# A state-space layer and a retrieval layer in one kernel: convolution inputs for two tiles at once, with W_in's columns stationary

## The reference

```python
zxbcdt = u @ W_in                                   # [4096, 2320]
z, xBC, dt = split(zxbcdt)                          # 1024, 1280, 16 columns
conv = conv_b
for i in range(4):                                  # causal convolution along the tokens
    conv = conv + pad(xBC)[:, i:i + s] * conv_w[i]
x, B, C = split(silu(conv))                         # 1024, 128, 128
dt = softplus(dt + dt_bias)
y = ssd(x * dt, -exp(A_log) * dt, B, C) + x * D     # scan over the tokens
y = rmsnorm(y * silu(z)) * norm_scale
x1 = layernorm(u + y @ W_out)
h = silu(x1 @ W_up.T + b_up) @ W_down.T + b_down    # 512 -> 2048 -> 256
sx, ix = top_k(first half of q(h) . keys, 8)        # 8 heads, 64 keys a half
sy, iy = top_k(second half of q(h) . keys, 8)
sc, experts = top_k(sx + sy, 8)                     # 64 experts a token
z = silu((h . down_embed[experts]) * softmax(sc))
out = layernorm(x1 + sum_k z_k * up_embed[experts_k])
```

## Time and profile before

| | |
|---|---|
| time, median of 3 runs | 3190.46 us (3180.9 to 3191.35) |
| span of the profiled execution | 3168.2 us |
| median less that span | 22.3 us |
| PE busy | 2818.4 us, 89% |
| DVE busy | 2783.2 us, 88% |
| ACT busy | 2105.8 us, 66% |
| POOL busy | 2098.0 us, 66% |
| gathers' share of the 16 DMA engines' span | 76.5% |

### The profile page before, as it was taken

One profiled execution on the slowest core, in us unless ns is written; L12 is line 12 of the kernel. 1 busy time (PEld: TensorE's weight loads), 2 busy tenths in 40 slices (PEclk: granted clock), 3 DMA queues, 4 the chain that ended last, 5 costly groups with the idle time before them and its releaser, 6 DMA issues.

```text
span 3168.2 us, 39919 instructions
## 1 busy us (share of the span) xinstructions
PE 2818.4 (89%) x9216; PEld 1501.1 (47%) x9216; DVE 2783.2 (88%) x10160; ACT 2105.8 (66%) x6641; POOL 2098.0 (66%) x2056
## 2 busy tenths in 40 slices
PE   7998999999899999999999999899899999998963
PEld 4444455545454545444445444444445454444431
DVE  3488999999989899999999899898999999898987
ACT  4476766767776667776666677666676666677642
POOL 0067666677667677666667767667766666766676
PEclk9999999999999999999999999999999999999986
DMA  8078888888888788888888888888888888888888
GB/s 289 16 265 277 276 270 269 274 283 289 275 270 267 261 282 293 279 281 269 269 275 300 263 277 280 265 268 291 270 278 275 271 275 290 282 279 275 269 296 280
DMA packets 189837, 856.45 MB, mean 270 GB/s; under 512 B 36192, under 2 KB 39392, under 8 KB 189088
## 3 DMA queue, kind: packets, MB, share of 16 engines
q0 software_dynamic: 163840, 805.44, 76.5%
q1 hardware_dynamic: 19104, 34.87, 3.2%
q10 hardware_dynamic: 6656, 13.60, 1.2%
HBM read 845.38 MB, written 8.39 MB: 269 GB/s over the span
## 4 chain that ended last, share of the span: by engine, by line
PE 57%; POOL 11%; DVE 10%; DMA 10%; ACT 6%; issue 6%; SPq 0%; DVEq 0%; ACTq 0%; POOLq 0%
PE bank L465 14%; POOL ring L279 11%; DMA ring<-embed,idx 10%; PE bank L508 8%; PE bank L362 7%; PE bank L481 6%; PE bank L342 5%; DVE bank L1166 4%; PE bank L496 4%; PE bank L444 3%; PE bank L371 3%; ACT xc L691 3%; DVE ring L1152 2%; PE bank L472 2%; ACT raw L688 1%
## 5 line engine op out<-in xcount | busy, mean ns | idle before, releaser
L279 POOL DMA_INDIRECT ring<-embed,idx x2048 | 2096.7, 1024 | 1057.9 <-issue 544.3
L1166 DVE SCALAR_TENSOR_TENSOR bank<-ring,coef,bank 128x512 f32<-128x512 f32 x1312 | 990.8, 755 | 7.4 <-issue 0.2
L1152 DVE SCALAR_TENSOR_TENSOR ring<-ring,hcur 128x256 f32<-128x256 f32 x2048 | 827.1, 423 | 185.7 <-DMA ring<-embed,idx 182.6
L508 PE MATMUL bank<-ring,diag_c 128*128 128x512 f32 x1344 | 668.8, 628 | 119.6 <-ACT diag_c L666 103.9
L657 ACT ACTIVATE coef<-prob,zp 128x1 f32<-128x1 f32 x2048 | 459.1, 293 | 456.1 <-DVE ring L1152 454.9
L465 PE MATMUL bank<-w_up,zs 128*128 128x512 f32 x1024 | 490.4, 630 | 69.2 <-ACT zs L779 65.8
L508 PEld LDWEIGHTS bank<-ring,diag_c 128*128 128x128 f32 x1344 | 246.6, 199 | 385.8 <-issue 224.9
L465 PEld LDWEIGHTS bank<-w_up,zs 128*128 128x128 f32 x1024 | 200.7, 201 | 329.7 <-issue 238.6
L997 DVE SCALAR_TENSOR_TENSOR xc<-raw,taps,xc 128x128 f32<-128x128 f32 x960 | 266.0, 351 | 53.8 <-ACT xc L691 53.8
L342 PE MATMUL bank<-w_in,ut 128*128 128x512 f32 (+1 forms) x768 | 285.1, 524 | 4.4 <-ACT seg L679 4.3
L666 ACT ACTIVATE diag_c<-cst,coef 128x128 f32<-128x128 f32 x672 | 234.8, 394 | 49.4 <-PE bank L508 38.9
(11 more groups left out here) (147 smaller groups left out, 3685.1 us busy)
## 6 DMA issues: line engine op xcount, KB each, us to landing
ring<-embed,idx POOLq DMA_INDIRECT x2048, 4.6
ring<-uT SPq DMA_DIRECT2D x4, 2048.0 KB, 14.3
ut<-uT SPq DMA_DIRECT2D x32, 256.0 KB, 6.5
zs<-u SPq DMA_DIRECT2D x32, 256.0 KB, 5.7
out<-acc SPq DMA_DIRECT2D x32, 256.0 KB, 4.7
w_up<-W_upT ACTq DMA_DIRECT2D x1, 4096.0 KB, 12.7
w_in<-W_in ACTq DMA_DIRECT2D x1, 2560.0 KB, 17.0
w_in<-W_in ACTq DMA_DIRECT2D x1, 2048.0 KB, 21.5
```

What stands on the lines that cost most here:

```text
L279: pool.indirect_dma_start(out=ring[:, k % RING, :], out_offset=None, in_=embed, in_offset=bass.IndirectOffsetOnAxis(ap=idx[:, half, k:k + ...
L508: m = pe.matmul(bank[SUM][:, :], diag_c[:, (len(PE_ROWS) * t + n) % DIAGS, :], ring[:, k % RING, DP:ROW], start=(n == 0), stop=(n == len(P ...
L1152: m = dve.scalar_tensor_tensor(out=ring[:, k % RING, 0:DP], in0=ring[:, k % RING, 0:DP], scalar=1.0, in1=hcur[:, :], op0=ALU.mult, op1=ALU ...
L1166: dve.scalar_tensor_tensor(out=total if n == len(DVE_ROWS) - 1 else running[:, :], in0=ring[:, k % RING, DP:ROW], scalar=coef[:, k:k + 1], ...
```

## The change

- xBC is computed for two tiles (256 tokens) at once, and directly with its columns on partitions: blocks of W_in are stationary and 256 columns of uT move. There are five parts of two blocks (x_part). Parts 0 and 1 of the tiles i+2 and i+3 are computed at the end of an even tile(i), parts 2, 3 and 4 at the start of the odd tile behind it. The turns and xbc_copy go.
- In even tiles state_in moves behind out_proj(0) and new(0) and waits for ACT's inputs of parts 0 and 1, whose banks it shares.
- The 45 taps of a pair become 15 steps of two instructions with 256 columns each, all in odd tiles; silu is applied to two tiles at once, and the copy of the last three columns stands behind it.
- Buffers are reused: xskip lies in raw, the picks' v1, v2, i1 and place in xdec, yT in seg, coef in zp, and the result of the back norm in total itself, which the store reads. The waits that this needs are added.
- uT is loaded for two tiles at once, when the last tile that used the one before has its z projection. The store of tile i-1 stands behind the load of u for tile i+1.
- dt_proj(3) and turn_dt(3) move into tile 0 behind key_scores, raw_dt(3) and softplus(1) behind numbers; the first gathers wait for dt_proj(3).
- Row 51, the fourth of group 16, is added by DVE instead of PE.

```diff
-PARTS = 3
+PARTS = 5
+NJ = NT // 2
+W2 = 2 * P
+EARLY = 2
-GROUPS = (..., "PPPD", "PP", "PDD", "PPPP", "D", "DDD", "PPPD", "D", "PDD")
+GROUPS = (..., "PPPD", "PP", "PDD", "PPPD", "D", "DDD", "PPPD", "D", "PDD")
+TAP_ORDER = [(p, j) for of in ((0, 1), (2, 3, 4)) for j in range(TAPS - 1) for p in of]
...
-            def load_ut(i):
-                sp.wait_ge(z_mm, 2 * i)
...
+            def load_ut(j):
+                sp.wait_ge(z_mm, 4 * j)
...
+            for i in range(NT):
+                if i % 2 == 0 and i // 2 + 1 < NJ:
+                    load_ut(i // 2 + 1)
+                if i + 1 < NT:
+                    load_u(i + 1)
+                if i > 0:
+                    store(i - 1)
...
+            pool.wait_ge(dt_mm, 2 * (NT // DTB))
             gathers(0, 0, True)
...
-            def xbc_proj(i, first, part):
-            def turn_xbc(i, first, part):
...
+            def x_part(j, part):
+                if part == 0:
+                    pe.wait_ge(ut_in, 16 * j + 16)
+                for n in range(2):
+                    c = DI + (2 * part + n) * P
+                    for k in range(KD):
+                        m = pe.matmul(bank[X_BANKS[part]][:, n * W2:(n + 1) * W2], w_in[:, k, c:c + P], uT_v[:, k, :],
+                                      start=(k == 0), stop=(k == KD - 1))
+                m.then_inc(xbc_mm, 1)
...
-            def state_in(i):
+            def state_in(i, early):
                 pe.wait_ge(dec_ok, 4 * i + 4)
+                if early:
+                    pe.wait_ge(tap_ok, PARTS * (i + 1) // 2 + EARLY)
...
# tile on PE
-                if ahead:
-                    xbc_proj(i + 1, False, 0)
...
-                    turn_xbc(i + 1, False, 2)
+                late = ahead and i % 2 == 1
+                early = i % 2 == 0 and i // 2 + 1 < NJ
+                if late:
+                    x_part((i + 1) // 2, 2)
+                    x_part((i + 1) // 2, 3)
                 turn_x1(i)
+                if late:
+                    x_part((i + 1) // 2, 4)
                 old(4, 5, 6)
...
                 old(18, 19)
-                if ahead:
-                    state_in(i + 1)
+                if early:
+                    x_part(i // 2 + 1, 0)
+                elif ahead:
+                    state_in(i + 1, False)
+                if ahead:
                     turn_y(i + 1)
+                if early:
+                    x_part(i // 2 + 1, 1)
                 old(20, 21)
                 if ahead:
                     out_proj(i + 1, False, 0)
                 new(0)
+                if early:
+                    state_in(i + 1, True)
                 if ahead:
                     out_proj(i + 1, False, 1)
...
# tile on ACT
-                if ahead:
-                    history(i + 1)
+                if late:
+                    inputs((i + 1) // 2, 2)
                 old(4)
-                if ahead:
-                    xbc_copy(i + 1, 0)
...
-                    inputs(i + 1, 0)
+                if late:
+                    inputs((i + 1) // 2, 3)
+                turn_x1(i)
                 old(5)
...
+                if late:
+                    inputs((i + 1) // 2, 4)
                 old(6)
...
                     state_decay(i + 1, range(NH // 2))
+                if early:
+                    inputs(i // 2 + 1, 0)
+                if ahead:
                     state_decay(i + 1, range(NH // 2, NH))
                     turn_y(i + 1)
+                if early:
+                    inputs(i // 2 + 1, 1)
...
# tile on DVE: taps_of(n, ...) runs steps of TAP_ORDER in odd tiles
+                old(4)
+                taps_of(0, 1)
+                old(5)
+                taps_of(2, 3)
+                old(6)
+                taps_of(4, 5)
                 old(7)
                 if ahead:
                     time_steps(i + 1)
+                taps_of(6, 7)
                 old(8)
+                taps_of(8, 9)
+                old(9)
+                taps_of(10, 11)
+                old(10)
+                taps_of(12)
+                old(11)
+                taps_of(13)
+                old(12)
                 private(i, first)
+                taps_of(14)
...
-                    dve.wait_ge(o_ok, t)
+                    dve.wait_ge(out_done, 16 * t + 16)
```

More of the change, by code:

```diff
@@ L246, in store @@
                 sp.wait_ge(o_ok, t + 1)
[L247 to L258, removed]
+                sp.dma_start(out[bass.ds(t, 1)].rearrange("t p c -> p (t c)"), total[:, :]).then_inc(out_done, 16)
+            for i in range(NT):
[5 more added lines that the diff above has]
+                    store(i - 1)
             store(NT - 1)
@@ L551, in tile @@
                 key_scores(i, 1)
+                if first:
+                    dt_proj(3)
+                    turn_dt(3)
                 if ahead:
@@ L579, in tile @@
                 new(1, 2, 3)
-            xbc_proj(0, True, 0)
-            xbc_proj(0, True, 1)
-            xbc_proj(0, True, 2)
-            turn_xbc(0, True, 0)
-            turn_xbc(0, True, 1)
-            turn_xbc(0, True, 2)
+            for part in range(PARTS):
+                x_part(0, part)
             pe.wait_ge(wz_in, 16)
@@ L597, in _ @@
             turn_dt(1)
-            state_in(0)
+            state_in(0, False)
             dt_proj(2)
@@ L683, in inputs @@
-            def inputs(i, b):
-                n = min(4, KC - 4 * b)
-                at = bank[XBC_BANKS[b]]
-                act.wait_ge(xbc_mm, 3 * i + b + 1)
-                act.activation(raw[:, 4 * b:4 * b + n, TAPS - 1:],
-                               at[:, 0:n * P].rearrange("p (a c) -> p a c", a=n), ACT.Copy).then_inc(raw_ok, 1)
-                for c in range(4 * b, 4 * b + n):
-                    m = act.activation(xc[:, c, :], at[:, (c % 4) * P:(c % 4 + 1) * P], ACT.Identity,
-                                       bias=cbias[:, c:c + 1], scale=taps[:, c, TAPS - 1:TAPS])
+            def inputs(j, part):
+                at = bank[X_BANKS[part]]
+                c0 = 2 * part
+                if part == 0 and j > 0:
+                    act.wait_ge(hist_ok, j)
+                    act.wait_ge(y_mm, 2 * j)
+                act.wait_ge(xbc_mm, PARTS * j + part + 1)
+                act.activation(raw[:, c0:c0 + 2, TAPS - 1:], at[:, :].rearrange("p (a c) -> p a c", a=2), ACT.Copy)
+                for n in range(2):
+                    m = act.activation(xc[:, c0 + n, :], at[:, n * W2:(n + 1) * W2], ACT.Identity,
+                                       bias=cbias[:, c0 + n:c0 + n + 1], scale=taps[:, c0 + n, TAPS - 1:TAPS])
@@ L861, in tile @@
                 turn_h(i)
+                if first:
+                    copy_dt(3)
                 if ahead:
@@ L898, in tile @@
                 new(3)
-            for b in range(3):
-                xbc_copy(0, b)
-            for b in range(3):
-                inputs(0, b)
+            for part in range(PARTS):
+                inputs(0, part)
             masked_steps(0, range(NH), True)
@@ L994, in convolve @@
                 else:
-                    dve.wait_ge(conv_ok, PARTS * (3 * i + j - 1) + part + 1)
-                for c in range(4 * part, min(4 * part + 4, KC)):
-                    m = dve.scalar_tensor_tensor(out=xc[:, c, :], in0=raw[:, c, j:j + P], scalar=taps[:, c, j:j + 1],
+                    dve.wait_ge(conv_ok, NTAP * i + TAP_AT[part, j - 1] + 1)
+                for c in range(2 * part, 2 * part + 2):
+                    m = dve.scalar_tensor_tensor(out=xc[:, c, :], in0=raw[:, c, j:j + W2], scalar=taps[:, c, j:j + 1],
                                                  in1=xc[:, c, :], op0=ALU.mult, op1=ALU.add)
@@ L1258, in tile @@
                 numbers(i)
+                if first:
+                    raw_dt(3)
+                    softplus(1)
                 if ahead:
@@ L1287, in _ @@
             time_steps(0)
-            for j in range(TAPS - 1):
-                for part in range(PARTS):
-                    convolve(0, j, part)
+            for part, j in TAP_ORDER:
+                convolve(0, j, part)
             dve.wait_ge(w_out_in, 16)
```

173 lines of the change are left out of this document (65 added, 108 removed).

## The result

The changed kernel takes 3205.1 us (median of 12 runs, 3188.6 to 3219.6), the kernel before 3190.9 in 12 runs beside it: a ratio of 1.0048, interval 1.0027 to 1.0069. It is half a per cent slower.

What follows compares the result with a forecast made beforehand. One loop through four engines, no engine alone, was taken to bound the kernel. A pair: -3.6 + 3.7 + 0 + 1.0 + 0.2 = +1.3 us; 15 pairs, +20 on the median 3190.5, gave 3210; range 3158 to 3245, the forecast's own 3200 to 3230.

Steps and rivals of the forecast that it cites:

- The signs that it named: Even tiles: new_state waits 3 to 4 us, DVE waits for gathers; odd: no DVE idle; periods near 91 and 99.
- Even tile, start: From the gather of row 15 to the start of private in even tiles: 3.6 us shorter.
- Even tile, end: After scan_gate in even tiles, new_state waits for the later state_in; the end of norm1 moves 3.7 us later.
- Odd tile, start: From norm1's end to private's start in odd tiles, DVE last: no change, between minus 1.5 and plus 0.8 us.
- PE's wait for h: PE waits 2 to 3 us for private's start, and half-speed work may follow: plus 1.0 us a pair.
- The moved row: Row 51's weigh, 0.76 us a tile on DVE, is hidden ahead of its wait for row 59: nothing.
- DMAs: ut's load, doubled, moves to the middle of even tiles: plus 0.2 us, between minus 1 and plus 0.7.
- Start and end: Tile 0's gain is taken back by softplus(1) on DVE; tiles 30 and 31 have no parts: 0, between -5 and +5.
- The base: Median 3190.5 us, to which the sum was added, with 22 us taken to lie around the profiled span of 3168.2.
- The shorter path wins: Rival: TensorE keeps 2.4 GHz through its wait, even tiles save 4.2 us; -2.0 a pair, 3160 us; chance 0.30.
- DVE sets the pace throughout: Rival: 60 taps become 30 of 0.41 us; -4.3 a pair, +1.5 for moved rows, 3148 us; chance 0.05.
- Saving and stall cancel: Rival: no clock term, +0.1 to +0.3 us a pair, 3194 us; chance 0.21.

Runs made afterwards that it cites:

- the first trace: The kernel before the change, unchanged, as first profiled: span 3168.2 us, where the median of its executions is 3190.9 us.
- The halves: Changed kernel with the first half of state_in put before x_part(0) and the second before x_part(1): 3139.9 us, ratio 0.9859 to the kernel before.
- the second trace: The kernel before the change, unchanged, traced once more: measured 3191.9 us, span 3190.0 us.
- the four matmuls: Changed kernel with four matmuls of 256 columns, result unread, on PE just before turn_h: 3158.4 us, ratio 0.9906 to the kernel before.

## Why the prediction was right, and where its steps were off

The forecast was 3210, the median is 3205. Against the first trace, from which its terms were read, the pair comes out as it said: -4.5 (even, Y to h) + 4.1 (odd, Y to N) - 0.5 (odd, N to h) + 2.2 (h to Y, both) = +1.3 us. The signs that it named came true, periods of 90.1 and 99.5 us for 91 and 99 among them; only new_state waits longer, 4.8 us (72.4/15) for the 3 to 4 named. But that the sum is met so closely is in part luck, as errors in several terms stood against each other.

*Even tile, start: right in kind, too small.* -3.6 was predicted from G to h; measured -3.8 (38.65, the mean of before, to 34.85), with 23 gathers in 29.24 us for the 29.7 taken. Besides, G was held fixed at Y + 13.5 (13.8 in the mean), and an earlier N was said to bring nothing; N came 0.8 us earlier and G moved to Y + 13.05. Y to h fell by 4.5, with DVE waiting for rows, as said.

*Even tile, end: right.* new_state was to wait and end near Y + 11.2, N at Y + 19.6; it ends at Y + 11.5, N is at Y + 19.9: +4.1 for +3.7, a little over its 4.0. The halves show the cause: with new_state back at Y + 5.4, 2.5 of the 4.1 are gone.

*Odd tile, start: right.* The up projection at N + 9.6 for 9.5, no idle time on DVE (0.05), N to h shorter by 0.5, inside the range. Four tap instructions in a row take 1.66 us, where four of 128 columns took 1.14: 0.13 more for each, which is the prediction's high end (0.135). The mean of 472 ns counts overlap.

*PE's wait for h: right in kind, half the size.* +1.0 was taken from ends of 0 and 3.4; h to Y grew by 2.2 a pair (1.5 against the second trace). The wait came out at 2.4 and 3.0 us as predicted, but the key products behind it were slow in each of the 14 odd rounds from 3 to 29, and in 5 of the 13 even ones. The value taken leaned on one tile of the earlier trace rows that showed no fall.

*The moved row:* zero, as predicted, in the changed kernel. *DMAs:* +0.2 can't be told apart; no run took it alone.

*Start and end: the start at the edge, the end left out.* 0, between -5 and +5, was predicted. h of tile 0 is 12.5 us earlier, softplus takes this back as said, and the Y of tile 1 comes 4.5 us later. (N of tile 1 comes 9.7 us later, but there the late state_in of tile 0 is in it, the wait of 7.0 above, and that belongs to the first of the 15 pairs.) What stands behind the last Y, of tile 31, had no term; it takes 175.6 us where the two traces of before have 171.7 and 170.8. Why was not followed.

*The base: wrong.* 22 us were put around the span. They are 1.8; the first trace was of an execution some 20 us below the median, with fewer slow up projections than the second. The change takes most of those slow stretches away, and an execution near the median has more of them to lose: against the second trace a pair gains 0.5 us instead of losing 1.3. From the Y of tile 1 to that of tile 31, all 15 pairs, the changed kernel takes 21 us more than the first trace (2847.0 for 2825.6), where +20 was forecast, and 1 us less than the second (2848.4). The two spans differ by 8.1 us all the same, by the start and the end. So of the loss of 14 us in the medians some 8 to 10 lie at the start and the end, and the pairs make up the rest, between -1 and +21 us with the execution that they are set against. The prediction put all of it in the pairs; that 3210 is near 3205 is luck to that extent.

*The rivals.* *The shorter path wins* needed the clock to stay up: the four matmuls did this, and the kernel took 3158 where the rival had 3160. That the two figures meet is luck: it also wanted a tap at its low end and +3.4 for state_in, and neither came. Left to itself the clock fell. *DVE sets the pace throughout* had its price nearly right, 65 us less of taps in 16 pairs, 4.1 a pair for 4.3, but even rounds leave DVE 6.6 us idle from N to h, and odd ones 5.6 us from Y to N. The Trainium skill, "VectorE: DVE Perf Modes", the section on the TRN2 errata, is borne out by the taps' busy time, 266.0 us in 960 instructions and 201.2 in 480; its advice of larger tiles did not carry to the time. *Saving and stall cancel*, 3194, is what the pairs did against the second trace; it lacked the start and the end.

## What to carry to other kernels

When a change makes two kinds of rounds out of one, cost each by its own last engine: work put at the end of one kind was paid in the next, and cutting a single step in halves turned 0.5% slower into 1.4% faster. Where PE will wait, count the products behind the wait at both clock levels, and ask which engine is made late upstream of it. Trace the base kernel twice before a sum of a few us a round is set against its median.

## What the runs showed of the hardware that was not expected

- Four matmuls that nobody reads, 1.7 us a tile, made the changed kernel 1.4% faster and the kernel before 0.65% slower; in the changed kernel the granted clock of the stretch behind a wait for h of 3.67 us was 0.64, and 1.00 behind one of 1.19.
- The length of one wait did not decide the fall alone: the key products took 3.60 us behind a wait of 2.8 us with the halves, and 4.35 us behind one of 2.2 us in the version with the four matmuls.
- Executions of the same kernel before differ by 22 us (spans 3168.2 and 3190.0) in part through how many of its up projections take 8.8 us for 7.1 behind the same wait of 2.19 us, 16 or 22 of 27; 0.66 of the clock was granted at the start of such a one.
